# A two-stage perceiver block: another order of the steps in both cross attentions

## The reference

```python
q = _split_heads(_layernorm(x) @ w_q.T + b_q)      # 256 rows per batch
k = _split_heads(ctx @ w_k.T + b_k)                # 4096 rows per batch
v = _split_heads(ctx @ w_v.T + b_v)
weights = softmax(q @ k^T / sqrt(16))
x = x + merge_heads(weights @ v) @ w_o.T + b_o
```

## Time and profile before

| | us |
|---|---|
| median of 3 runs | 4365.25 |
| lowest, highest | 4364.61, 4373.9 |
| span of the profiled execution | 4357.8 |
| TensorE busy | 3998.4 |
| VectorE busy | 3011.4 |
| ScalarE busy | 2806.9 |
| GpSimd busy | 1811.5 |

### The profile page before, as it was taken

How to read it: one execution, slowest core, us unless ns; L and a number is a source line. 1 busy time by engine, 2 the same in 40 slices (tenths; PEclk the granted TensorE clock), 3 DMA queues, 4 the chain that set the end, 5 groups by cost and what they waited for, 6 DMA issues and landing times. The chain is left out here.

```text
span 4357.8 us, 81373 instructions
## 1 busy us (share of the span) xinstructions
PE 3998.4 (92%) x30320; PEld 2853.4 (65%) x30320; DVE 3011.4 (69%) x6897; ACT 2806.9 (64%) x5769; POOL 1811.5 (42%) x1862
## 2 busy tenths in 40 slices
PE   4999999988979999999999999967999999976998
PEld 3555555545757787887888888854555555535777
DVE  4777777767777767767677676644787877767745
ACT  2777777677967767777676776723676767654322
POOL 3333333204556555555556555523322322202644
PEclk7999999999989999999999999988999999988999
DMA  6666665536020110010100101027666666512265
GB/s 167 119 118 118 115 110 114 103 50 217 1 78 5 35 35 28 25 37 26 37 25 25 37 25 39 13 54 154 115 114 113 115 113 112 99 27 72 85 191 186
DMA packets 208194, 354.02 MB, mean 81 GB/s; under 512 B 26927, under 2 KB 110564, under 8 KB 205745
## 3 DMA queue, kind: packets, MB, share of 16 engines
q1 hardware_dynamic: 200217, 338.42, 35.4%
q0 software_dynamic: 7584, 10.39, 0.7%
HBM read 257.48 MB, written 114.98 MB: 85 GB/s over the span
## 5 line engine op out<-in xcount | busy, mean ns | idle before, releaser
L759 DVE TENSOR_REDUCE xa_m_part<-xa_unit 128x2 f32<-128x1024 f32 x1024 | 1247.7, 1224 | 515.3 <-PE xa_unit L907 513.8
L683 ACT ACTIVATE xa_ex<-xa_unit 128x1024 f32<-128x1024 f32 x1024 | 1029.8, 1019 | 259.7 <-PE xa_unit L891 254.4
L921 PE MATMUL xa_pv<-xa_ex,xa_vs 128*17 128x256 f32 x8192 | 546.5, 383 | 7.1 <-ACT xa_ex L683 7.0
L907 PE MATMUL xa_unit<-xa_ks,xa_q_base 48*128 48x512 f32 x2048 | 437.9, 425 | 117.8 <-ACT xa_ex L683 85.8
L1068 POOL TENSOR_SCALAR lt_p<-lt_p,lt_stat 128x192 f32<-128x192 f32 x384 | 355.3, 926 | 453.6 <-DVE lt_stat L1058 453.0
L891 PEld LDWEIGHTS xa_unit<-xa_q_base,xa_ks 50*128 50x128 f32 x4096 | 312.1, 185 | 316.2 <-issue 242.5
L891 PE MATMUL xa_unit<-xa_q_base,xa_ks 50*128 50x256 f32 x4096 | 502.5, 324 | 10.2 <-DVE xa_m_part L759 6.1
L1911 PE MATMUL lt_bank<-lt_wp,lt_xt 128*128 128x512 f32 x1728 | 465.1, 411 | 14.3 <-DVE lt_wp L1748 6.3
L1078 ACT ACTIVATE lt_p<-lt_p,lt_stat 128x128 f32<-128x128 f32 (+1 forms) x768 | 321.7, 420 | 157.2 <-DVE lt_stat L1053 154.5
L1911 PEld LDWEIGHTS lt_bank<-lt_wp,lt_xt 128*128 128x128 f32 x1728 | 314.5, 192 | 78.8 <-DVE lt_xt L1741 9.1
L618 POOL TENSOR_SCALAR xa_m_neg<-xa_m_blk 128x8 f32<-128x8 f32 x128 | 29.9, 233 | 780.4 <-DVE xa_m_blk L770 780.4
(11 more groups left out here) (334 smaller groups left out, 7903.3 us busy)
## 6 DMA issues: line engine op xcount, KB each, us to landing
xa_ks<-keys SPq DMA_DIRECT2D x372, 256.0 KB
keys<-xa_kp SPq DMA_DIRECT2D x128, 512.0 KB, 3.3
xa_cx<-in_ctx_t SPq DMA_DIRECT2D x64, 512.0 KB
lt_u<-in_lt_wqkv SPq DMA_DIRECT2D x54, 256.0 KB
places<-in_moe_blank SPq DMA_DIRECT2D x47, 258.0 KB, 8.6
moe_xs<-places SPq DMA_DIRECT2D x47, 258.0 KB
lt_w<-in_lt_w SPq DMA_DIRECT2D x6, 1536.0 KB
xa_q_base<-xa_m_rows SPq DMA_DIRECT2D x512, 2.0 KB
```

What stands on the lines that cost most here:

```text
L683: act.activation(x.ex[:, n % x.NE, :, :], x.place_of[step][:, :, :].rearrange("p o (j s) -> p (o j) s", j=2), ACT.Exp).then_inc(*x.ex_done ...
L759: dve.tensor_reduce(x.m_part[:, i % 2, qt, 2 * pair:2 * pair + 2, ch:ch + 1], x.place_of[step][:, :, :], AX.X, ALU.max).then_inc(*x.dve_ou ...
L907: mm = pe.matmul(bank[:, odd, :], x.q_base[rows, pair, b * S + qt * P:b * S + (qt + 1) * P], x.ks[unit % x.NU][rows, pair % 4, ch * 512:(c ...
L921: mm = pe.matmul(x.pv[32 * j:32 * j + x.VW, 0:S], x.vs[:, i % x.NV, kt, 4 * g + j, :], x.ex[:, n % x.NE, 2 * (j % 2) + j // 2, :], start=( ...
```

## The change

The two-slot loop is replaced by a written order of a quad, 32 tokens, and the lead by a list of its own.

- A quad is S S W W W S S M J S M C M W W W X S M G S M C W W M S M J C M. W of quad q starts three slots behind its scores (`BEHIND` = 3), so the first run of three ends the quad before. J is a job, C a `combine`, G `max_rows` q+1, `gather` q-2 and, in even quads, `stack_k` q/2 + 2. X is `turn_out` or `project_out` in a batch's third and fourth quad after its end, or a query job.
- The lead: the keys and values of item 0 come before the first maximum, with `stack_k` 1 after the keys. Then 18 maxima, with `max_rows` 0 after the 11th and one key job of item 1 after the 9th, 12th, 15th and 18th.
- The queries of batches 1 to 3 leave the lead: their two jobs are the X of quads 5 and 7 of the batch before, and `stack_q` follows the second.

```diff
-    LEAD = 18
+    LEAD, ROWS_AT = 18, 11
+    AHEAD = (9, 12, 15, 18)
+    ORDER, BEHIND = ("S S W W W S S M J S M C M W W W X S M G S M C W W M S M J C M").split(), 3
...
+        for step in self.keys(0, 1) + [("value", 0, t) for t in range(self.KT // 2)]:
+            out += self.follow(step)
+            if step == ("key", 0, 1, 1):
+                out.append(("stack_k", 1))
...
+        for b in range(B):
+            extra[per_batch * (b + 1) + 2], extra[per_batch * (b + 1) + 3] = ("turn_out", b), ("project_out", b)
+            if b + 1 < B:
+                extra[per_batch * b + 5], extra[per_batch * b + 7] = ("query", b + 1, 0), ("query", b + 1, 1)
...
+        while top < self.LEAD:
+            out += maximum()
+            top += 1
+            if top == self.ROWS_AT:
+                out.append(("max_rows", 0))
+            if top in self.AHEAD:
+                out += self.follow(jobs.pop(0))
+        for quad in range(quads + 4):
+            scores, weighs, parts = 8 * quad, 8 * quad - self.BEHIND, 0
...
+            for token in self.ORDER:
+                if token == "M" and top < total:
+                    out += maximum()
+                    top += 1
...
+                elif token == "G":
+                    if quad + 1 < quads:
+                        out.append(("max_rows", quad + 1))
+                    if 0 <= quad - 2 < quads:
+                        out.append(("gather", quad - 2))
+                    if quad % 2 == 0 and quad // 2 + 2 < 2 * self.ITEMS:
+                        unit = quad // 2 + 2
...
+                        out.append(("stack_k", unit))
+                elif token == "J" and jobs and self.may_fill(jobs[0], scores):
+                    out += self.follow(jobs.pop(0))
+                elif token == "X" and quad in extra:
+                    out += self.follow(extra.pop(quad))
```

More of the change, by code:

```diff
@@ L344, in filling, with follow @@
         values = lambda i: [("value", i, t) for t in range(self.KT // 2)]
-        queries = lambda b: [("query", b, mt) for mt in range(2)]
-        first = values(0)
-        out = self.keys(0, 1) + first[0:2] + queries(1) + first[2:4] + queries(2) + queries(3)
+        out = []
         for i in range(1, self.ITEMS):
             out += self.keys(i, 0) + self.keys(i, 1) + values(i)
+        return out
+    def follow(self, step):
+        out = [step]
+        if step[0] == "value" and step[2] % 2 == 1:
+            m = 2 * (step[1] + 1) + step[2] // 2
+            out += [("split", m)] if m < 2 * self.ITEMS else []
+            out += [("ctx", m + 2)] if m + 2 < 2 * self.ITEMS else []
+        if step[0] == "query" and step[2] == 1:
+            out.append(("stack_q", step[1]))
         return out
@@ L362, in steps @@
         out += [("ctx", 2), ("ctx", 3), ("late",)]
-        total = self.SLOTS * self.ITEMS
-        batch = self.SLOTS * self.NKB
-        jobs = self.filling()
[L366 to L390, removed]
-                if step[0] == "value" and step[2] % 2 == 1:
-                    m = 2 * (step[1] + 1) + step[2] // 2
-                    out += [("split", m)] if m < 2 * self.ITEMS else []
-                    out += [("ctx", m + 2)] if m + 2 < 2 * self.ITEMS else []
-                if step[0] == "query" and step[2] == 1:
-                    out.append(("stack_q", step[1]))
-            unit, at_u = divmod(t + 32, 16)
-            if at_u == 0 and 2 <= unit < 2 * self.ITEMS:
-                out.append(("stack_k", unit))
-            if t == 2 - self.LEAD:
-                out.append(("stack_k", 1))
-            if quad >= 2 and at >= 2:
-                b, kb = divmod((quad - 2) // 4, self.NKB)
-                if kb == self.NKB - 1 and b < B:
-                    out.append(("combine", b, (quad - 2) % 4, at // 2 - 1))
@@ L406, in steps @@
-        assert not jobs and not outputs
+        for step in self.keys(0, 1) + [("value", 0, t) for t in range(self.KT // 2)]:
+            out += self.follow(step)
+            if step == ("key", 0, 1, 1):
+                out.append(("stack_k", 1))
+        total, quads = self.SLOTS * self.ITEMS, 4 * self.ITEMS
+        per_batch = 4 * self.NKB
+        jobs = self.filling()
+        extra = {}
+        for b in range(B):
+            extra[per_batch * (b + 1) + 2], extra[per_batch * (b + 1) + 3] = ("turn_out", b), ("project_out", b)
+            if b + 1 < B:
+                extra[per_batch * b + 5], extra[per_batch * b + 7] = ("query", b + 1, 0), ("query", b + 1, 1)
@@ L407, in steps @@
+        assert not jobs and not extra and top == total
         return out
```

18 lines of the change are left out of this document (added).

## The result

The changed kernel takes **4621.28 us** (median of 4 runs, 4616.27 to 4628.0); the kernel before took 4367.53 us beside it (4 runs, 4364.61 to 4373.9). The ratio is **1.0574**, with a 95% interval of 1.0561 to 1.0587. The direction was forecast, the size was not: +63 us were expected and +254 came, outside the range of 4345 to 4480.

The account below looks back on a forecast made before the run. The order of TensorE's queue and its waits were taken as the bound. Per stage, steady part +25, queries +36, end +2 and lead -30 or -33 gave +33 and +30: +63 on 4365.25, 4428 us, range 4345 to 4480.

Parts of the forecast that it names:

- Order alone: Steady quads of both cross attentions: with no transfer late, a quad takes 13.13 us for 14.03 before.
- The stack lands at 26.1 for 24.1: Every second quad: TensorE's seventh maximum, due at 24.10 us, waits 2.0 us for the key stack.
- The pair 28.5 to 29.0: Two successive steady quads: 28.5 us, or 29.0 where jobs are keys, against 28.06 before.
- Combining and output turns: Combining quads and output turns: 4 us per stage, partly hidden in new waits; nothing to 1 us for each of 16 quads.
- Query quads: Query's second part, quad 7: staging write and query stack delay the next rows of maxima, +12 us, three times per stage.
- The lead: Before the steady quads: first scores at about 70.7 us, quad 1 earlier by 30 us, in the second stage 32.7.
- The end of a stage: Last quads, without jobs: 12.4 us each, as now 12.3, and one more late stack, +2 us per stage.
- rival 1: Steady quads: the stack doesn't bind, quads take 13.13 us; -43 and -46 us per stage, 4276 us, chance 0.12.
- rival 2: Query quads: the wait is small, 4 instead of 12 us six times, -48 us, 4380 us; chance 0.10.
- rival 3: Lead: doesn't shrink because unit 1's stack or chunk writes take the queries' place; +63 us, 4491 us, chance 0.08.
- rival 4: Steady quads: order worse than walked, quads 13.8 us, +0.5 us a pair, 4457 us; chance within the forecast's 0.70.
- the skill's rule: Transfer queue: small transfers can complete before large earlier ones; pairs of 28.5 us everywhere, 14 us less in both stages, 4414.

Follow-up runs that it names:

- experiment 3: Changed kernel with each key-stack transfer bringing only 512 of 1024 columns from the fourth unit on: ratio 1.0293 to the kernel before.
- experiment 8: Changed kernel with rows of maxima and key stack early in the quad, gather left in place, combining steps after it: ratio 1.0048 to the kernel before.
- experiment 2: Changed kernel with only the first combining step moved behind G and the next run of weighings: ratio 1.0453 to the kernel before.
- experiment 7: Changed kernel with five extra, unread matrix products on TensorE ahead of each unit's first maximum: ratio 1.0627 to the kernel before.
- experiment 6: Changed kernel with the first combining step behind the side transposes and key stacks of half the columns from unit 3: ratio 1.0183 to the kernel before.
- experiment 4: Changed kernel with the key stack alone moved behind the quad's first maximum, ahead of the rows of maxima: ratio 1.1145 to the kernel before.
- experiment 5: Changed kernel with the six query jobs of batches 1 to 3 back in the lead, none in quads: ratio 1.0547 to the kernel before.
- experiment 1: Changed kernel with G and the first J exchanged in the quad's order: ratio 1.0087 to the kernel before.
- experiment 9: Early rows of maxima and key stack, late gather, plus VectorE's side work moved into its idle time: 4284.85 us, ratio 0.9879 to the kernel before.

## Why the prediction was right in sign and wrong in size

- **Order alone, 13.13 us a quad**: right, 13.24 measured. Without stacks in the way (experiment 3) quads 10 to 13 of a batch take 14.0, for VectorE's two small steps and ScalarE's exp behind them (experiment 8); this was left out. In the even quads it is 5 us a stage; in the odd ones it lies partly in the wait for the stack.
- **The stack lands at 26.1 for 24.1, a wait of 2.0 us in each odd quad**: right in place and on the average in size, 27.6 us for 16 waits in 120 to 900. That each is near 2.0 is not so: 2.39, 2.10, 3.24 and 1.32 us in the first four, and 1.92, 1.36, 0.49 and 2.01 in another execution of the same steps (experiment 2). The stack took 14.7 us from its issue (117.41) to its landing (132.1), where 13.9 was read off.
- **The pair 28.5 to 29.0**: failed. The step that failed is the sentence that puts 2.3 to 2.4 us behind the wait as if TensorE went on at full speed. After most of the waits it goes on at 1.2 GHz: 1.33 us more in quad 3, from experiment 7. Odd quads were 16.7 for 15.6.
- **Combining and output turns, +4 us (bounds 0 to 16)**: the main failure, 46 us in the combining quads and 6 in the output quads. Its bounds came from the lengths of VectorE's steps, 2.6 us a quad. What was not asked is what the first of them waits for in its new place: the copy of the sums that TensorE's transposes, eight tokens further on in the same quad, make possible: 2.74 us in each of the twelve quads, and the low clock behind it. Experiment 2 takes this wait away: 40 us less in the combining quads.
- **Query quads, +12 us each**: right, 11.9 over the other odd quads (28.6 for 16.7), by the chain that was described: from quad 6's first scores (168.37) to those of quad 8 (209.21) it is 40.8 us for 41.0.
- **The lead, -30 and -32.7 us**: -24.7 and -25.2. The first scores are at 75.24 for the 70.7 walked. The stack was issued at 56.19 where the walk had about 52, so the maximum of index 16 waited for it until 71.07 (66 in the walk), and the job behind it took 2.87 us at the low clock. Two rows of the lead show it:

```profile
71.07 1.22 PE L931 MATMUL xa_unit<-xa_ks,xa_q_base 48*128 48x512 f32 x4 [10.19 <-DMA xa_ks<-keys]
72.22 2.87 PE L887 MATMUL xa_side<-xa_cxp,xa_wp 128*128 128x512 f32 x6
```

- **The end of a stage, +2**: 13.1 measured in the first; it has combining quads too.
- **The rivals**: none came. Odd quads as short as rival 1's 13.1 exist only where the stack is small (13.3, experiments 3 and 6); rival 2's small waits are refuted by three of about 11 us, rival 3 (the lead doesn't shrink) by 92.35, and rival 4's slow order by 13.24. Rival 1's sum is also a few us off its own terms (-47, +36 and -30 are -41, not -43), which changes nothing. The small transfers that were to profit by the skill's rule do not (experiment 4). The range missed because its bounds came from the transfers' times and the lengths of VectorE's steps; neither a wait for the gather nor the clock was in them.
- **By stage**: the first cross attention was to take 33 us more and takes 132.4, the second, with the way to it, 30 and takes 120.4. The same errors stand in both, and 9.3 us lie behind the last copy.

The sum again with what the runs showed, for the first stage's 57 quads: 860 forecast, 46 for the multiplication's wait and the clock behind it, 18 in the odd quads, for the clock above all (their waits were 1.8 us on the average, not longer than forecast), 10 in the even quads (about half for the weights' small steps, most of the rest for the low clock that runs on from the quad before), 6 and 3 for outputs and queries, 943. The 6 and the 3 were read off, not explained.

## What to carry to other kernels

When a step is moved within a hand-written order, ask for each engine's queue what it now **waits for** at that place, not only how long it takes: 0.73 us of VectorE's work cost 3 to 4 us a quad because its input was made later in the same quad. Put a step behind the event that feeds it by at least one operation of its engine, and into a place where that engine idles anyway.

A wait of TensorE isn't priced at its own length. Look at the granted clock in stretches of a few us behind each wait, since it doesn't fall after each; if it falls, the work behind it costs up to twice, and short waits that come back in every quad cost more than they show. To fill such a wait with work that has to be done anyway can be worth more than its length (experiment 7).

Compare the kernel stage by stage on marks that both versions have. Only so could two errors of the sum, and a trade at par (experiment 5), be told from one big number. And take the length of a single quad from more than one execution: quad 5 differed by 5.3 us between two traces of the same steps.

## What the runs showed of the hardware

- TensorE's granted clock falls to 1.2 GHz after many of the waits of 1.2 to 3.3 us in a stretch that is otherwise busy, and stays there until some 4 to 10 us after the wait. What a wait costs beside its own length goes with that time: 0.1 us in quad 1 (15.76 less 13.24 and 2.39), where the clock stayed at 1.00; 1.65 in quad 3 (16.99 less 13.24 and 2.10), with 3.4 us at the lower level; and 2.7 in quad 21 (18.88 less 13.24, 2.21 and 0.7 for its query job), with 6.9 us. After the waits of 0.83 to 0.97 us (quads 27, 29 and 45) it stayed at 1.00. What makes the difference wasn't tried.
- A VectorE addition with both operands in SBUF took 2.73 to 2.81 us beside a GpSimd subtraction (experiment 1, three times) and 0.69 without one; a maximum, which reads PSUM, took its usual 1.23 us beside the same subtraction (at 303.07 in the changed kernel). The Trainium skill (SBUF — State Buffer, SBUF: two separate sides) says that VectorE and GpSimd share one pair of ports as an exclusive lock, which fits.
- Six transfers of 256 KB, each into 16 rows of the key tile, kept the transfer engines busy for some 14 us, at about 121 GB/s while nothing was queued behind them (the stretch 150 to 152 us of the changed kernel below), where the write of 512 KB ran at 391 GB/s.

```profile
150.00:152.00 2.00, 2.00 (x34) 1.12 (x27) 0.56 (x1) 1.96 (x4) 1.92 (x2) 1.00 1.03 121
```

- What follows the second stage's last copy of the sums, in which all these kernels are the same, took 449 to 451 us in experiments 1 and 9 and 483 to 484 us in 6 and 8, which ran on another chip; the kernel before differed by about as much between chips (4334.66 and 4337.19 beside 1 and 9, 4371.8 beside 6 and 8). Differences of spans between chips are therefore not laid to the change.
